# First cross-attention: query and output products between score halves, biases as bf16 rows, separate maxima per half

## The chip, the cores and the metric

The kernel runs on one core of a Trainium2 chip. The metric is the device time of one execution in microseconds (us). Engines are named as in the profile: PE is TensorE (matmul), PEld its weight loads, DVE is VectorE, ACT is ScalarE, POOL is GpSimd, SP issues the transfers.

## The reference

The program is a Perceiver-like stack of four layers, each a cross-attention, a self-attention and a feed-forward block. The change touches the first block alone, a quantised cross-attention with 16 heads of 16 channels. The 16x64 rows of x (1024) attend to all 16x128 rows of the context (2048), in one batch:

```python
q = (x @ Wq + bq).reshape(1, B * N, H, hd)
kv = (cond @ Wkv + bkv).reshape(1, -1, 2, H, hd)
q = _fq_sym(q * scale, axis=-1)       # round to 127 steps, per row and head
k = _fq_sym(k, axis=-1)
v = _fq_sym(v, axis=2)                # per channel, over all keys
attn = softmax(einsum('bhqd,bhkd->bhqk', q, k))
attn = _fq_unsigned(attn, axis=-1)    # round to 255 steps of the row's maximum
out = einsum('bhqk,bhkd->bhqd', attn, v)
return out @ Wp + bp
...
x = x + _L0_xattn_ref(_layernorm(x, axis=-1), ctx_2048, ...)
```

## The kernel before

The block `l0_xattn` fills the first 500 us of the program. Each engine runs a program of its own, in the order in which the code issues it; semaphores ("signals" in the code) order the engines against each other. Nothing is reordered by a scheduler.

**Start (to 76 us).** PE makes the values (`values`) and then the keys in 8 sets (`keys`, L1082 to L1089). Each half of a set begins with a product of a row of ones and the bias row `bk`, both fp32, that puts the bias in PSUM; two fp32 products with `wk` are added. DVE rounds the keys, POOL splits them into three bf16 parts (L1299 to L1306), PE transposes the parts, ACT copies them into `kT`. After its first work POOL has nothing to do until the first rounded set.

**Scores (76 to 486 us).** The 1024 rows are 8 tiles of 128 rows. A tile goes through 16 heads, and a head's scores are 128x2048, in one PSUM tile `s_ps` of two halves. Each engine's `tile_steps` runs a loop over i = 0 to 15; tile 0 and the last tile stand outside the hardware loop, and differ in what they leave out. In step i:

- PE: `score(t, i + 1)` makes the two halves of the next head, two 512-column products each (L1139). A half may be overwritten when DVE has taken the same half of the head before (`scores_taken`). Then `mix(t, i - 4)` multiplies the transposed weights of a head by its values, 16 small products (L1147). Behind that, in certain steps, stand products of the neighbouring tiles: `turn_out(t-1)` (i=5), `project_out(t-1)` and the transposition of the next tile's normalised rows (i=7), `queries(t+1)` (i=9), `turn_queries(t+1)` (i=13). Those with a bias begin with the fp32 product of ones and the bias row.
- DVE: `take_scores(t, i + 1)` copies each half to `ex` and takes its maximum (L1413 and L1416; each is followed by a readout of the accumulator, which is what signals `scores_taken`). The second pass starts its maximum from the first one's result `first_max`, so it waits for the first pass's own readout (`dve.wait_ge(scores_taken.sem, ...)` just ahead of it). Around the passes stand the works for other tiles: `totals` (i=1), `divide_out` (i=4), the next tile's layer norm (i=4 and 6), `add_out` (i=8), `round_queries` (i=11). Each ends with a wait for its own result, ahead of the next pass.
- POOL: `shift` makes the bias of the exponential, one operation on 128x1 (L1319); in step 5 it also makes the next tile's 1/sqrt(var).
- ACT: one exponential of 128x2048 per head (L1238), and copies: the transposed queries (`take_queries`, after heads 14 and 0), the transposed output (6), the normalised rows (8).
- SP: one transposing DMA per head moves the rounded weights (`pb`) to `pt`; `ex`, `pb` and `pt` have four slots each.

## Time and profile before

| | us |
|---|---|
| median of 3 runs | 3743.81 |
| lowest, highest | 3738.99, 3747.11 |
| the profiled execution | 3749.25 |
| its span | 3747.5 |
| the block of the change, from the profile | 0 to 500 |
| of it the eight tiles | 77.1 to 486 |

Over the whole span PE is busy 81%, DVE 61%, ACT 40%, POOL 14%. These shares average blocks with different limits, and say nothing on this one. The chain of work that ended last holds only the last 0.6 us, since it breaks at the ends of blocks. So the tiles are read from the list of groups by line, the waits, the stretches of single tiles and the order of time. All eight tiles have the same pattern. The profiled execution's time is 1.75 us longer than its span, and 5.4 us above the median of the runs. In the section with the rows, a row of a stretch gives its ends, its length, the busy time of PE, PEld, DVE, ACT and POOL with their instructions, PE's granted clock as a share of full speed, the share of the DMA engines and GB/s.

### The profile page before, as it was taken

The numbers are of one execution on the slowest core, as the hardware profiler recorded it, in microseconds if no ns is written. First come the engines' busy times: TensorE is split into PE (matmuls) and PEld (weight loads), VectorE is DVE, ScalarE is ACT, GpSimd is POOL, SyncE is SP. The second block draws the span as 40 slices with busy tenths as digits, with TensorE's granted clock in tenths as the row PEclk, the third lists the DMA queues.
The fourth block names the chain that finished last, engine by engine and source line by source line (L and its number), as shares of the span: only waits on it lengthen the run. The fifth ranks groups of instructions, "written<-read, shape, count | busy, mean of one in ns | idle before, by whom it ended". The sixth has DMA issues, their size and how long they took to land. (4 is left out here: it accounts for less than half of the span.)

```text
span 3747.5 us, 63586 instructions
## 1 busy us (share of the span) xinstructions
PE 3031.9 (81%) x23988; PEld 2108.2 (56%) x24036; DVE 2278.8 (61%) x4830; ACT 1506.0 (40%) x3074; POOL 535.2 (14%) x791
## 2 busy tenths in 40 slices
PE   7677789988776888857996868789898978787878
PEld 3333368867664556534664435355555556676767
DVE  6888844442558888865655732367777754444453
ACT  4777721111346455443442112155545532223332
POOL 3101000000002222111110022222212111111000
PEclk8766689988887776768998979899999988898787
DMA  4877740000010000010002040000000021000000
GB/s 125 164 159 164 160 135 0 0 22 0 14 56 2 2 2 2 2 69 9 6 12 69 0 135 22 3 4 3 3 6 3 3 87 51 1 0 0 1 1 12
DMA packets 316495, 141.38 MB, mean 38 GB/s; under 512 B 296221, under 2 KB 305953, under 8 KB 312613
## 3 DMA queue, kind: packets, MB, share of 16 engines
q1 hardware_dynamic: 308072, 138.45, 13.7%
q8 instruction: 126, 2.06, 0.2%
q10 hardware_dynamic: 8256, 0.52, 0.2%
q14 instruction: 41, 0.34, 0.0%
HBM read 67.65 MB, written 3.15 MB: 19 GB/s over the span
## 5 line engine op out<-in xcount | busy, mean ns | idle before, releaser
L1238 ACT ACTIVATE l0x_pb<-l0x_ex,l0x_neg_max,l0x_q_scale 128x2048 uint16<-128x2048 f32 x128 | 267.8, 2093 | 108.2 <-POOL l0x_neg_max L1319 106.5
L1139 PE MATMUL l0x_s_ps<-l0x_kT,l0x_qT 128*128 128x512 bf16 x466 | 206.5, 539 | 111.3 <-DVE l0x_ex L1416 51.8
L1413 DVE TENSOR_SCALAR_CACHE_REDUCE l0x_ex<-l0x_s_ps 128x1024 f32<-128x1024 f32 x128 | 156.4, 1222 | 46.1 <-PE l0x_s_ps L1139 35.0
L1416 DVE TENSOR_SCALAR_CACHE_REDUCE l0x_ex<-l0x_s_ps,l0x_first_max 128x1024 f32<-128x1024 f32 x128 | 164.3, 1284 | 16.7 <-DVE l0x_ex L1413 0.5
L1139 PEld LDWEIGHTS l0x_s_ps<-l0x_kT,l0x_qT 128*128 128x128 bf16 x512 | 39.2, 111 | 204.8 <-DVE l0x_ex L1416 140.5
L263 PE MATMUL l3x_bank<-l3x_w_kv_x,l3x_ctxT 128*128 128x512 f32 x256 | 120.1, 613 | 26.6 <-ACT l3x_ctx_k L762 15.8
L1147 PEld LDWEIGHTS l0x_o_ps<-l0x_v,l0x_vT 128*128 128x128 f16 x2048 | 78.6, 104 | 59.1 <-issue 41.8
L2198 PEld LDWEIGHTS l1a_bank<-l1a_u,l1a_gm 64*64 64x64 f32 x2048 | 95.5, 194 | 15.6 <-issue 14.8
L2190 PE MATMUL l1a_bank<-l1a_r,l1a_r 32*64 32x64 f32 x2048 | 75.9, 287 | 35.0 <-DVE l1a_r L2532 33.6
L263 PE MATMUL l2f_bank<-l2f_w,l2f_ln_yT 128*128 128x352 f32 x256 | 103.5, 539 | 0.0
L2198 PE MATMUL l1a_bank<-l1a_u,l1a_gm 64*64 64x8 f32 x2048 | 98.4, 235 | 4.7 <-DVE l1a_gm L2551 4.7
L2179 PE MATMUL l1a_bank<-l1a_steps,l1a_after 128*128 128x512 f32 x128 | 99.1, 866 | 0.0
L2190 PEld LDWEIGHTS l1a_bank<-l1a_r,l1a_r 32*64 32x64 f32 x2048 | 69.4, 166 | 46.6 <-DVE l1a_r L2532 37.9
L3681 PE MATMUL l3x_bank<-l3x_wproj,l3x_cat 128*128 128x256 bf16 x768 | 91.9, 278 | 4.1 <-DVE l3x_cat L3553 4.1
L679 DVE SCALAR_TENSOR_TENSOR l2f_moe_act<-l2f_bank,l2f_moe_cw,l2f_moe_sg 128x176 f32<-128x176 f32 x64 | 24.9, 400 | 114.8 <-ACT l2f_moe_sg L664 114.3
L263 PEld LDWEIGHTS l3x_bank<-l3x_w_kv_x,l3x_ctxT 128*128 128x128 f32 x256 | 46.6, 192 | 81.2 <-issue 56.7
L2191 PE MATMUL l1a_bank<-l1a_r,l1a_r 32*64 32x64 f32 x2048 | 76.6, 264 | 13.3 <-issue 13.1
L707 PE MATMUL l3x_bank<-ident,l3x_rows 128*128 128x128 f32 x448 | 64.4, 281 | 27.6 <-ACT l3x_rows L755 27.6
L3681 PEld LDWEIGHTS l3x_bank<-l3x_wproj,l3x_cat 128*128 128x128 bf16 x768 | 74.7, 100 | 20.9 <-issue 6.7
L1319 POOL TENSOR_SCALAR l0x_neg_max<-l0x_mx,l0x_q_neg 128x1 f32<-128x1 f32 x128 | 34.0, 265 | 346.6 <-DVE l0x_ex L1416 321.3
L1147 PE MATMUL l0x_o_ps<-l0x_v,l0x_vT 128*128 128x16 f16 x2048 | 75.2, 174 | 5.8 <-DMA l0x_vT<-l0x_pb 5.8
L654 PE MATMUL l2f_bank<-l2f_w,l2f_moe_actT 128*128 128x256 f32 (+1 forms) x256 | 78.6, 408 | 0.0
(747 smaller groups left out, 7838.0 us busy)
## 6 DMA issues: line engine op xcount, KB each, us to landing
l2f_wproj_raw<-in_L_xattn_wproj SPq DMA_DIRECT2D x2, 2048.0 KB, 12.3
l3a_w<-in_L_attn_W SPq DMA_DIRECT2D x4, 1024.0 KB, 11.3
l2f_w<-in_L_ffn_w SPq DMA_DIRECT2D x1, 2816.0 KB, 11.6
l0x_ex<-in_ctxT SPq DMA_DIRECT2D x8, 256.0 KB, 5.0
l0a_wq<-in_L_attn_W_Q SPq DMA_DIRECT2D x1, 2048.0 KB
l0a_wk<-in_L_attn_W_K SPq DMA_DIRECT2D x1, 2048.0 KB
l0x_vT<-l0x_pb SPq DMA_TRANSPOSE x128, 3.6
l0a_wv<-in_L_attn_W_V SPq DMA_DIRECT2D x1, 2048.0 KB, 7.8
```

The costliest lines, as they stand in the source:

```text
L263: ins = nc.tensor.matmul(out, wT(c), rhs(c), start=start and n == 0, stop=stop and n == chunks - 1)
L654: ins = nc.tensor.matmul(self.y, self.actT[0:w, e % 2, n, :], self.w_out[0:w, e, n, :], start=(e == 0 and n == 0), stop=(e == E - 1 and n ...
L1139: ins = mm(s_ps[:, j * 512:(j + 1) * 512], qT[:, h, :], kT[:, h // 2, j * 512:(j + 1) * 512], start=True, stop=True)
L1147: ins = mm(o_ps[:, h * HD:(h + 1) * HD], pt[:, h % 4, j * P:(j + 1) * P], vv[:, j, h * HD:(h + 1) * HD], start=j == 0, stop=j == KT - 1)
L1238: s.activation(pb[:, h % 4, :], ex[:, h % 4, :], ACT.Exp, scale=q_scale[:, h:h + 1], bias=nb[:, h:h + 1], accum_out=sums[:, h:h + 1]).then ...
L1413: v.tensor_scalar(ex[:, h % 4, 0:1024], s_ps[:, 0:1024], 1.0, None, ALU.mult, ALU.max, accum_out=first_max[:, h:h + 1]).then_inc(o.up(scor ...
L1416: v.tensor_scalar(ex[:, h % 4, 1024:2048], s_ps[:, 1024:2048], 1.0, first_max[:, h:h + 1], ALU.mult, ALU.max, accum_out=mx[:, h:h + 1]).th ...
L2179: ins = mm(bank[4 + j][:], after[:], flat(steps_[:, 8 * j:8 * j + 8, :]), start=False, stop=True)
L2190: mm(out, r1[0][r, 8 * half + j, tok], r1[1][r, 8 * half + j, tok], start=True, stop=False)
L2191: ins = mm(out, r2[0][r, 8 * half + j, tok], r2[1][r, 8 * half + j, tok], start=False, stop=True)
L2198: ins = mm(bank[6][r, h * HP:(h + 1) * HP], gm[r, h, :], u[r, h * HP:(h + 1) * HP], start=True, stop=True)
L3681: ins = nc.tensor.matmul(y_bank, cat[:, 8 * (n % 2) + c, :], wproj[:, 8 * n + c, i, :], start=n % 2 == 0 and c + i == 0, stop=n % 2 == 1 a ...
```

## The change

**Order.** In `score` the caller can hand in a generator that is advanced once after each half. `queries(t+1)` goes between the halves of head 8 (step i=7, before i=9 behind the mix), `project_out(t-1)` between the halves of head 10 (i=9, before i=7 behind the mix). The transposition of the next tile's rows moves from i=7 to i=3, `turn_queries` from 13 to 10. On DVE the norm moves from (4, 6) to (0, 2), `round_queries` from 11 to 8, `add_out` from 8 to 11; on ACT the norm's copy moves from 8 to 4 and the copy of the first half of the queries from 14 to 12; on POOL the norm moves from 5 to 1.

**Maxima.** The two passes write `low_max` and `high_max`, and the second doesn't wait for the first. POOL's `shift` becomes two operations on 128x1, the second waiting for the first.

**Waits.** The works between the DVE passes no longer wait for their own last result; `divide_out` waits for `totals_ready` instead.

**Biases.** The three bias vectors come as one array of 3x768 fp32 (six weight transfers in place of eight). POOL splits it at the start into three bf16 rows whose sum is the bias, in 11 operations on 3x768, and PE waits for them ahead of the first keys. Each bias product becomes one of bf16 with three rows.

```diff
+    for dst, name in ((wv, "Wv"), (bv, "bv"), (b3, "b3"), (wk, "Wk"), (wq, "Wq"), (wp, "Wp")):
...
-                mm(misc[:, 0:D], env.ones_row[:, 0:P], bq[:], start=True, stop=False)
-                project(nc, misc[:, 0:D], lambda c: norm.yT[:, c, :], lambda c: wq[:, c, :], DC, start=False).then_inc(q_ps.sem, 1)
+                mm(misc[:, 0:D], ones3[:], bq, start=True, stop=False)
+                for c in reversed(range(DC)):
+                    ins = mm(misc[:, 0:D], norm.yT[:, c, :], wq[:, c, :], start=False, stop=c == 0)
+                    if c == 0:
+                        ins.then_inc(q_ps.sem, 1)
+                    yield
...
+            pe.wait_ge(biases_set.sem, biases_set.value())
...
                     ins.then_inc(scores_ps.sem, 1)
+                    if between is not None:
+                        next(between)
...
+                    between = queries(t + 1) if more and i == 7 else project_out(t - 1) if before and i == 9 else None
...
+            for n in range(3):
+                src = b_sum if n else b3
+                pool.sem_inc(first.up(), 1)
+                g.tensor_copy(b_part[:], src[:]).then_inc(first.up(), 1)
+                pool.wait_ge(first.sem, first.at())
+                if n < 2:
+                    g.tensor_tensor(b_sum[:], src[:], b_part[:], ALU.subtract).then_inc(first.up(), 1)
+                    pool.wait_ge(first.sem, first.at())
+                pool.sem_inc(first.up(), 1)
+                g.tensor_scalar(b_part[:], b_part[:], env.ident[0:3, n:n + 1], 0.0, ALU.mult, ALU.add).then_inc(first.up(), 1)
...
-                g.tensor_scalar(nb[:, h:h + 1], mx[:, h:h + 1], q_neg[:, h:h + 1], LN255, ALU.mult, ALU.add).then_inc(o.up(shifted), 1)
+                g.tensor_scalar(mx[:, h:h + 1], low_max[:, h:h + 1], high_max[:, h:h + 1], q_neg[:, h:h + 1], ALU.max, ALU.mult).then_inc(o.up(), 1)
+                pool.wait_ge(o.sem, o.at())
+                pool.sem_inc(o.up(), 1)
+                g.tensor_scalar(nb[:, h:h + 1], mx[:, h:h + 1], 1.0, LN255, ALU.mult, ALU.add).then_inc(o.up(shifted), 1)
...
-                dve.wait_ge(scores_taken.sem, scores_taken.value(t, 2 * h + 1))
-                v.tensor_scalar(ex[:, h % 4, 1024:2048], s_ps[:, 1024:2048], 1.0, first_max[:, h:h + 1], ALU.mult, ALU.max, accum_out=mx[:, h:h + 1]).then_inc(o.up(scores_taken), 1)
+                v.tensor_scalar(ex[:, h % 4, 1024:2048], s_ps[:, 1024:2048], 1.0, None, ALU.mult, ALU.max, accum_out=high_max[:, h:h + 1]).then_inc(o.up(scores_taken), 1)
...
-                o.eng.wait_ge(tile_done.sem, o.at(tile_done))
```

How PE's order moves is read from three places in the looped tile. First, PE before, in steps 7 to 9: the score products of head 8 are the first row, L1158 and the L263 behind it are `project_out`, L241 the transposition of the normalised rows, L1102 and its L263 `queries`.

```order
L1139 MATMUL l0x_s_ps<-l0x_kT,l0x_qT 128x512 x2
L1147 MATMUL l0x_o_ps<-l0x_v,l0x_vT 128x16 x16
L1158 MATMUL l0x_t_ps<-l0x_bp,ones_row 128x256
L263 MATMUL l0x_t_ps<-l0x_wp,l0x_oT 128x256 x2
L239 REGISTER_ALU
L241 MATMUL l0x_misc<-ident,l0x_ln_y 128x128 x2
L1135 REGISTER_ALU
L1139 MATMUL l0x_s_ps<-l0x_kT,l0x_qT 128x512 x2
```

Everything of the neighbouring tiles stands in a row behind the mix, ahead of the first half of head 9. PE after, in step 7 (L1105 and L1107 are `queries`, L1146 the score products, L1156 the mix):

```order
L1146 MATMUL l0x_s_ps<-l0x_kT,l0x_qT 128x512 x2
L1105 MATMUL l0x_misc<-l0x_b_rows,l0x_ones3 128x256
L1107 MATMUL l0x_misc<-l0x_wq,l0x_ln_yT 128x256
L1142 REGISTER_ALU
L1146 MATMUL l0x_s_ps<-l0x_kT,l0x_qT 128x512 x2
L1107 MATMUL l0x_misc<-l0x_wq,l0x_ln_yT 128x256
L1156 MATMUL l0x_o_ps<-l0x_v,l0x_vT 128x16 x16
```

The bias and one product stand behind the first half, the other product behind the second. `project_out` has the same form in step 9. DVE before, the two passes of a head with what each waits for:

```order
L1413 TENSOR_SCALAR l0x_ex,l0x_first_max<-l0x_s_ps 128x1024 [waits l0x_scores_ps]
L1414 REGISTER_ALU
L1416 TENSOR_SCALAR l0x_ex,l0x_mx<-l0x_s_ps,l0x_first_max 128x1024 [waits l0x_scores_taken,l0x_scores_ps]
L1427 TENSOR_TENSOR l0x_o_rows<-l0x_o_ps,l0x_total 128x256 [waits l0x_mixed]
L1409 REGISTER_ALU [waits l0x_o_ready]
```

And DVE after, at the same place:

```order
L1443 TENSOR_SCALAR l0x_ex,l0x_low_max<-l0x_s_ps 128x1024 [waits l0x_scores_ps]
L1444 REGISTER_ALU
L1445 TENSOR_SCALAR l0x_ex,l0x_high_max<-l0x_s_ps 128x1024 [waits l0x_scores_ps]
L1456 TENSOR_TENSOR l0x_o_rows<-l0x_o_ps,l0x_total 128x256 [waits l0x_totals_ready,l0x_mixed]
L1439 REGISTER_ALU
```

The wait for `scores_taken`, a result of DVE itself, is gone from the second pass, and the wait for `o_ready` from behind the division.

## Rows read from the trace of the kernel before

**Rows 1.** Stretches: tile 0, first and sixth of the looped tiles, last tile.

```profile
77.10:124.70 47.60, 32.79 (x253) 12.79 (x256) 42.08 (x74) 35.10 (x34) 5.18 (x19) 0.72 0.83 162
124.70:178.30 53.60, 38.50 (x339) 19.12 (x344) 43.47 (x77) 37.94 (x42) 5.17 (x19) 0.69 0.73 155
...
387.90:442.00 54.10, 41.55 (x339) 19.67 (x344) 43.47 (x77) 38.24 (x42) 5.17 (x19) 0.63 0.68 155
442.00:486.00 44.00, 31.11 (x354) 15.33 (x356) 40.55 (x68) 36.11 (x38) 4.01 (x15) 0.81 0.92 184
```

**Rows 2.** Order of time, DVE in tile 2: start us, duration, what, [idle before].

```profile
186.75 1.22 DVE L1413 TENSOR_SCALAR_CACHE_REDUCE l0x_ex<-l0x_s_ps 128x1024 f32<-128x1024 f32 x1
187.90 0.08 DVE L1413 DVE_READ_ACCUMULATOR l0x_ex<-l0x_s_ps 128x1 f32 x1
188.11 1.28 DVE L1416 TENSOR_SCALAR_CACHE_REDUCE l0x_ex<-l0x_s_ps,l0x_first_max 128x1024 f32<-128x1024 f32 x1
...
189.32 1.22 DVE L1413 TENSOR_SCALAR_CACHE_REDUCE l0x_ex<-l0x_s_ps 128x1024 f32<-128x1024 f32 x1
...
192.53 1.23 DVE L1413 TENSOR_SCALAR_CACHE_REDUCE l0x_ex<-l0x_s_ps 128x1024 f32<-128x1024 f32 x1 [0.23 <-DVE l0x_o_rows L1427]
```

**Rows 3.** Waits of the six looped tiles: total us, times, longest us.

```profile
DVE l0x_ex L1413 <- PE l0x_s_ps L1139: 23.1, 19, 2.5
...
PE l0x_s_ps L1139 <- ACT l0x_qT L1210: 13.2, 6, 2.4
```

**Rows 4.** Order of time, PE's score products beside rows 2.

```profile
186.89 1.03 PE L1139 MATMUL l0x_s_ps<-l0x_kT,l0x_qT 128*128 128x512 bf16 x2 [0.39 <-DVE l0x_ex L1416]
...
188.19 1.01 PE L1139 MATMUL l0x_s_ps<-l0x_kT,l0x_qT 128*128 128x512 bf16 x2
```

**Rows 5.** Order of time, PE and DVE at the end of tile 2.

```profile
225.00 1.53 PE L1139 MATMUL l0x_s_ps<-l0x_kT,l0x_qT 128*128 128x512 bf16 x3
...
226.10 1.23 DVE L1413 TENSOR_SCALAR_CACHE_REDUCE l0x_ex<-l0x_s_ps 128x1024 f32<-128x1024 f32 x1 [0.70 <-PE l0x_s_ps L1139]
...
230.32 1.22 DVE L1413 TENSOR_SCALAR_CACHE_REDUCE l0x_ex<-l0x_s_ps 128x1024 f32<-128x1024 f32 x1 [1.56 <-PE l0x_s_ps L1139]
```

**Rows 6.** Order of time, the query products in tile 2, lower clock.

```profile
208.82 1.13 PE L1102 MATMUL l0x_misc<-l0x_bq,ones_row 1*128 1x256 f32 x2
...
209.88 2.08 PE L263 MATMUL l0x_misc<-l0x_wq,l0x_ln_yT 128*128 128x256 f32 x4
...
211.74 1.91 PE L1139 MATMUL l0x_s_ps<-l0x_kT,l0x_qT 128*128 128x512 bf16 x4
...
212.84 1.22 DVE L1413 TENSOR_SCALAR_CACHE_REDUCE l0x_ex<-l0x_s_ps 128x1024 f32<-128x1024 f32 x1 [2.44 <-PE l0x_s_ps L1139]
```

**Rows 7.** Order of time, the query products in tile 0, upper clock.

```profile
105.65 1.13 PE L263 MATMUL l0x_misc<-l0x_wq,l0x_ln_yT 128*128 128x256 f32 x4
```

**Rows 8.** POOL's operation on 128x1, from the page.

```profile
L1319 POOL TENSOR_SCALAR l0x_neg_max<-l0x_mx,l0x_q_neg 128x1 f32<-128x1 f32 x128 | 34.0, 265 | 346.6 <-DVE l0x_ex L1416 321.3
```

**Rows 9.** POOL's groups by line and shape: busy us, mean ns, idle before.

```profile
L3589 POOL TENSOR_TENSOR l3x_wproj<-l2f_wproj_raw,l3x_wproj 128x1024 bf16<-128x1024 f32 x8 | 17.0, 2122 | 0.6
L1301 POOL TENSOR_TENSOR l0x_k_rest<-l0x_k_num,l0x_k_parts 128x512 f32<-128x512 f32 x8 | 9.2, 1154 | 0.6
...
L3587 POOL CAST l3x_wproj<-l2f_wproj_raw 128x1024 bf16<-128x1024 f32 x8 | 8.3, 1042 | 0.5
...
L1304 POOL CAST l0x_k_parts<-l0x_k_rest 128x512 bf16<-128x512 f32 x8 | 4.9, 610 | 1.3 <-POOLq L1303 1.3
```

**Rows 10.** Order of time, POOL in the start.

```profile
9.99 0.56 POOL L232 TENSOR_TENSOR l0x_ln_rstd<-l0x_ln_ve,neg_half 128x1 f32<-128x1 f32 x1
```

**Rows 11.** Order of time, the first keys.

```profile
26.55 0.69 PE L1087 MATMUL l0x_s_ps<-l0x_bk,ones_row 1*128 1x256 f32 x2
...
30.03 0.69 DVE L1355 TENSOR_REDUCE l0x_k_row<-l0x_s_ps 128x32 f32<-128x512 f32 x1 [1.58 <-PE l0x_s_ps L263]
```

**Rows 12.** A small operation of DVE among the keys: min/median/max ns.

```profile
L1357 DVE TENSOR_SCALAR l0x_k_row<-l0x_k_row x8: 180/239/1105, 30.8 to 64.9; 128x32 f32<-128x32 f32 x8
```

**Rows 13.** The first score pass by line: min/median/max ns.

```profile
L1413 DVE TENSOR_SCALAR_CACHE_REDUCE l0x_ex<-l0x_s_ps x128: 1218/1224/1226, 77.1 to 483.3; 128x1024 f32<-128x1024 f32 x128
```

More of the change, by code:

```diff
@@ L1086, in keys @@
                     out, first = k_bank[n % 2][:, b * D:(b + 1) * D], n * CH + b * SC
-                    mm(out, env.ones_row[:, 0:P], bk[:], start=True, stop=False)
+                    mm(out, ones3[:], bk, start=True, stop=False)
                     ins = project(nc, out, lambda c: ctxT[:, c, first:first + SC], lambda c: wk[:, c, :], DC, start=False)
@@ L1118, in _ @@
                 if n == 2:
-                    queries(0)
+                    whole(queries(0))
                 if n >= 2:
@@ L1127, in _, with score @@
             pe.wait_ge(qT_taken.sem, qT_taken.value(0))
-            def score(t, h, first=False):
+            def score(t, h, first=False, between=None):
                 if not first and h % 8 == 0:
@@ L1157, in project_out @@
                 pe.wait_ge(oT_taken.sem, oT_taken.value(t))
-                mm(out_bank[:, D:2 * D], env.ones_row[:, 0:P], bp[:], start=True, stop=False)
-                project(nc, out_bank[:, D:2 * D], lambda c: oT[:, c, :], lambda c: wp[:, c, :], DC, start=False).then_inc(y_ps.sem, 1)
+                mm(out_bank[:, D:2 * D], ones3[:], bp, start=True, stop=False)
+                for c in reversed(range(DC)):
+                    ins = mm(out_bank[:, D:2 * D], oT[:, c, :], wp[:, c, :], start=False, stop=c == 0)
+                    if c == 0:
+                        ins.then_inc(y_ps.sem, 1)
+                    yield
             def tile_steps(t, before, more):
                 for i in range(H):
+                    between = queries(t + 1) if more and i == 7 else project_out(t - 1) if before and i == 9 else None
                     if i + 1 < H:
-                        score(t, i + 1)
+                        score(t, i + 1, between=between)
                     elif more:
@@ L1172, in tile_steps @@
                         mix(t - 1, H + i - 4, before)
+                    if more and i == 3:
+                        pe.wait_ge(qT_taken.sem, qT_taken.value(t))
+                        whole(norm.tensor(pe, t + 1, misc))
                     if before and i == 5:
                         turn_out(t - 1)
-                    if before and i == 7:
-                        project_out(t - 1)
-                    if more and i == 7:
-                        whole(norm.tensor(pe, t + 1, misc))
-                    if more and i == 9:
-                        queries(t + 1)
-                    if more and i == 13:
+                    if more and i == 10:
                         turn_queries(t + 1)
@@ L1193, in _ @@
             turn_out(last)
-            project_out(last)
+            whole(project_out(last))
         @block.scalar
@@ L1256, in tile_steps @@
                         take_queries(o, 1)
-                    if before and i == 6:
-                        take_out(o, t - 1)
-                    if more and i == 8:
+                    if more and i == 4:
                         o.t = t + 1
@@ L1262, in tile_steps @@
                         o.t = t
-                    if more and i == 14:
+                    if before and i == 6:
+                        take_out(o, t - 1)
+                    if more and i == 12:
                         act.wait_ge(qT_ps.sem, qT_ps.value(t + 1))
```

51 lines of the change are left out of this document (30 added, 21 removed).

## The prediction

> **What bounds the kernel now.** I read the stretches first, one per tile. Tile 0 takes 47.6 us, the six looped tiles 317.3 us together (124.7 to 442.0), which is 52.9 us each, and the last 44.0 us [rows 1]. In a looped tile DVE is busy 43.5 us and no other engine more. The reader is to see two things in that row: DVE is the fullest engine, and 9.4 us of the tile are not DVE work.
>
> The order of time of DVE shows a plain head, one with nothing else in it [rows 2]: the first pass starts at 186.75 and the next head's first pass at 189.32, so 2.57 us per head. The first pass starts its readout 1.15 us after its own start (187.90), which ends at 187.98; the second pass starts only at 188.11, 1.36 us after the first. From there to the next first pass are 1.21 us: nothing stands between those two, and that pass starts together with the readout. Sixteen plain heads are 41.1 us. So 11.8 us of a looped tile are insertions of DVE and waits.
>
> DVE's insertions: of the 43.5 us busy, 16 heads of 2.44 us (1.23 from 186.75 to 187.98, and 1.21) are 39.0, which leaves 4.5 us, and after each of five insertions DVE idles 0.23 us until its own result has come back (192.53) [rows 2]. The list of waits shows the rest: the first pass waits 23.1 us in six tiles for a score product, 3.9 us a tile, and PE in turn waits 13.2 us for ACT's copy of the queries, 2.2 a tile [rows 3].
>
> **The change part by part.** All of it is summed against the profiled execution, 3749.25 us.
>
> *The two passes.* Without the wait the second pass can start as the first one's readout does, 1.15 us after the first, as the first pass does behind the second. Its duration of 1.28 us becomes the first one's 1.22, since it takes the same form; so its readout comes at 1.15 in place of 1.21. DVE alone then needs 2.30 us for a head, 0.27 less. What is late next is PE. I work out its loop at the lower of its clock's two levels, 1.2 GHz. A second-half product starts at 186.89, 0.06 us after the readout that frees its half; the mix follows, and the next first-half product starts at 188.19, 1.30 us later [rows 4]. A product started at 225.00 lets the pass start at 226.10, 1.10 us later [rows 5]. Around the loop: first pass to its successor 1.15, that one's readout and release 1.15 + 0.08 + 0.06, product to product 1.30, product to pass 1.10: 4.84 us for two heads, 2.42 us for one. At the upper level, 2.4 GHz, the products take half, and DVE's 2.30 stands. The granted clock was 0.69 in the first looped tile and 0.63 in the sixth [rows 1], so about a third of the time at the upper level: 2.38 us per head. It hides nothing else; PE's slack is gone at the lower clock, and each product inserted on PE there is paid in full.
>
> *The waits behind the insertions.* Five per looped tile by 0.23 us is 1.15 us less. With the gaps inside the insertions (their operations still wait for each other) DVE's own additions become about 4.7 us a tile: 4.5 busy, 1.0 of gaps that stay, less 0.8 by which neighbours overlap their ends, 0.07 us each.
>
> *The queries.* Before: bias 1.13 us and products 2.08 us by their records, at the lower clock, and the first pass behind them is 2.44 us late. By starts (208.82 for the bias, 211.74 for the next score product) they hold PE 2.9 us [rows 6]. After: the bias is one bf16 pass of 256 columns, which I price at half a score product (four end 1.91 us after the first one's start [rows 6], some 0.43 each), 0.2 us; the products stay at four passes, 1.7. Between the halves they delay the second-half product by 0.75 us (3.20 in place of 2.45 after the head's start), and the second product and the mix delay the next first half; together I get 1.6 us late at the lower clock. At the upper clock the four product passes end 1.13 us after the first one's start [rows 7], two of them about 0.5: that between halves fits in the 1.15 us of a pass, so nothing is late.
>
> *The output product* has the same size, and now stands in the step where DVE runs `round_queries` (2.0 us) between two passes. PE has then 2 us of slack: nothing is late in the looped tiles. In the last tile nothing covers it, and it costs like the queries, up to 1.6 us. `add_out`, one step later, doesn't wait.
>
> *The smaller PE insertions.* `turn_queries` makes the pass 0.70 us late now [rows 5]; behind it `add_out` stands on DVE, 0.4 us, so 0.4 remains at the lower clock. `turn_out` has lost the layer norm that covered it: 0.5. The transposition in step 3 lies beside `divide_out`: 0.05. Upper clock: nothing. So the waits for PE come to 2.5 us a tile at the lower clock and 0 at the upper, 1.7 for a third at the upper.
>
> *The copy of the queries* at head 12 in place of 14 comes two heads before it is needed. The pass that was 1.56 us late [rows 5] is on time. What else waits on ACT: a head takes ACT 2.1 us, and the tile's 38.3 us busy [rows 1] fit in 44. Nothing is late on SP, whose transfers are moved past by none of the edits.
>
> *POOL's second operation* costs 0.27 us by its like [rows 8] and a wait of 0.1 to 0.3, once per head, in the chain DVE, POOL, ACT, transfer, mix. That chain has four slots. I take it at nothing for the tiles: the cover is the three heads, 7 us, between the exponential and the pass that needs its slot. At the very end it shows once, 0.4 us, against 0.9 us that the bf16 bias saves in the last output product.
>
> A looped tile after: 16 x 2.38 + 4.7 + 1.7 = 44.5 us in place of 52.9. Six save 50.4. Tile 0: 16 x 2.38 is 38.1, and 0.8 + 0.2 for the norm, 1.1 queries, 1.8 rounding, 0.5 turning: 42.5 in place of 47.6, 5.1 saved. The last: 38.1 + 0.5 + 0.5 + 1.1: 40.2, 3.8 saved. Tail 0.5.
>
> *The start.* POOL's 11 operations have no row at 3x768. The nearest are casts (0.61 at 512 columns, 1.04 at 1024) and two-input operations (1.15 and 2.12) [rows 9]; midway, 0.83 and 1.64. Four copies, four two-input and three scaled ones of either price are 12.4 to 14.8 us, with ten gaps 13.2 to 15.6. At the 512 prices all would be 9.4, at 2.12 for each 23.3. POOL is free at 10.6 [rows 10], so the biases are ready at 24 to 26.3, and the keys start at 26.55 [rows 11]: just in time. Then two short biases bring the first rounding, for which DVE waited at 30.03, 0.6 us forward. I take 0.6 gained; the ends are 0.6 gained and 7.5 lost (34.0 less 26.5). Two fewer transfers I take at nothing.
>
> Sum: 50.4 + 5.1 + 3.8 + 0.5 + 0.6 = 60.4 us, so 3688.9 against the profiled execution. That one is 5.4 us above the median of the runs, so against the median: 3743.8 - 60.4 = **3683.4 us**, a saving of 1.6%.
>
> **The rivals.** *Upper clock.* Denser products keep PE at the upper level: a looped tile is 16 x 2.30 + 4.7 = 41.5 us, 11.4 less, in all about 80: 3664. For it: plain heads come closer together. Against it: the fp32 bias passes go, and the granted clock was 0.63 to 0.72 in tiles with more of them [rows 1]. The Trainium skill, "TensorE: Matmul & The Clock Gate", section "What's actually happening", says that the clock is low by default and that activity lifts it; by that rule this rival is possible, and its opposite too.
>
> *Lower clock throughout.* 16 x 2.42 + 4.7 + 2.5 = 45.9: 42 + 4 + 3 + 1 = 50 saved, 3694.
>
> *The head's time stays at 2.57*, because the product of the second half, not the readout, sets the second pass: at 186.89 + 1.10 = 187.99 it was ready for the pass of 188.11, only 0.12 us before [rows 2, 4]. Then 128 x 0.19 = 24 us of the gain are missing: 3707.
>
> *The biases are late* by up to 7.5 us in place of 0.6 gained: 3691.
>
> *Slower.* POOL now works twice per head beside the passes. If a pass waited while POOL holds something that both need, each of the two operations would add 0.27: 128 x 0.54 = 69 us, 3752. It decides from 0.47 us per head (60.4 / 128). For it: among the keys a small DVE operation takes 180 to 1105 ns [rows 12], the long ones beside POOL's two-input work. Against it: all 128 first passes lie within 1218 and 1226 ns [rows 13], though POOL's operation falls into each. The Trainium skill, "SBUF — State Buffer", section "Who interferes with whom", names this lock between the two engines, but excepts the form of operation that also writes an accumulator; by that rule, which agrees with the 8 ns spread, the passes are safe and only small operations are not.
>
> **How the numbers follow.** Forecast with the mixed clock 0.55; upper clock 0.14; lower throughout 0.12; head's time stays 0.10; biases late 0.05; slower 0.04. A measurement of this kernel can tell about 0.2%, 7.5 us. All but the last are faster: 0.95; within 0.2% 0.01; slower 0.04. The forecast's own spread is some 10 us, a third of the clock's share either way and the unknown gaps; the range of 3664 to 3708 takes in all cases but the slower one, its ends being the upper clock and the unchanged head.
>
> **What would show it.** In the changed profile: plain heads 2.30 to 2.42 us apart, the second pass 1.15 us behind the first and 1.22 long; no wait of PE for ACT's copy at the tile's end; DVE's wait for the score products near 1.7 us a tile, most of it at the head with the queries; looped tiles of 42 to 46 us; POOL's last bias operation done before 26.5. It is wrong if the second pass is still 1.3 us behind, if the tile is above 47, or if time appears outside the first 500 us, where nothing is touched.

## The result, and the profile after

The changed kernel takes 3694.07 us (median of 4 runs, 3688.57 to 3697.23) against 3742.96 for the kernel before on the same chip: a ratio of 0.9867, 95% interval 0.9854 to 0.9880, 48.9 us saved. The profiled execution took 3693.92 us with a span of 3692.1; between the two profiled executions the span fell by 55.4 us. That is 6.5 us more than the medians say, since the profiled execution of the kernel before was 6.3 us above its median and that of the changed kernel 0.2 below. The forecast was 60.4 saved and 3683.4 us. The time lies in the range and on the right side, but two of the prediction's steps failed in opposite directions, as the experiments show.

The first group is from the page of the kernel after: the span, and the granted clock in 40 slices (tenths of full speed).

```profile
span 3692.1 us, 63817 instructions
...
PEclk8899799988977777679998798899999988898787
```

Each slice is 92 us, so the first attention is the first four to five. Next its stretches, one per tile: tile 0, the first, third and sixth of the looped tiles, the last one (busy us and instructions of PE, PEld, DVE, ACT and POOL, then granted clock, DMA share, GB/s). They answer to [rows 1].

```profile
74.90:115.80 40.90, 30.58 (x255) 11.80 (x253) 39.88 (x74) 32.06 (x32) 9.19 (x32) 0.79 0.93 160
115.80:159.10 43.30, 31.16 (x343) 14.37 (x344) 40.64 (x79) 38.89 (x42) 10.71 (x38) 0.90 1.15 187
200.60:241.60 41.00, 30.25 (x342) 15.29 (x342) 40.57 (x78) 37.59 (x42) 9.94 (x35) 0.92 1.10 205
...
323.60:364.60 41.00, 30.34 (x342) 15.29 (x342) 40.57 (x78) 37.60 (x42) 9.94 (x35) 0.92 1.11 208
364.60:405.50 40.90, 30.57 (x325) 13.20 (x325) 38.41 (x70) 37.66 (x39) 9.21 (x33) 0.83 1.13 196
```

From the third on a looped tile takes 41.0 us, the first two 43.3 and 41.5; before all six took 52 to 54. DVE is busy for 40.57 of the 41.0, so it now has hardly a gap. The granted clock is 0.92 (0.90 and 0.86 in the first two) where it was 0.63 to 0.70, and PE's records add up to 30 us where they were 37 to 42. The eight tiles together take 330.6 us in place of 408.9.

DVE's order of time in the third looped tile answers to [rows 2]: start, duration, what.

```profile
227.57 1.22 DVE L1443 TENSOR_SCALAR_CACHE_REDUCE l0x_ex<-l0x_s_ps 128x1024 f32<-128x1024 f32 x1
228.72 0.08 DVE L1443 DVE_READ_ACCUMULATOR l0x_ex<-l0x_s_ps 128x1 f32 x1
228.72 1.22 DVE L1445 TENSOR_SCALAR_CACHE_REDUCE l0x_ex<-l0x_s_ps 128x1024 f32<-128x1024 f32 x1
229.86 0.08 DVE L1445 DVE_READ_ACCUMULATOR l0x_ex<-l0x_s_ps 128x1 f32 x1
229.86 1.22 DVE L1443 TENSOR_SCALAR_CACHE_REDUCE l0x_ex<-l0x_s_ps 128x1024 f32<-128x1024 f32 x1
```

The second pass starts with the first one's readout, 1.15 us behind it, and takes 1.22; the next head follows after 1.14: 2.29 us for a head. All waits of DVE in the six looped tiles (total us, times, longest) answer to [rows 3]:

```profile
DVE l0x_ex L1443 <- PE l0x_s_ps L1146: 2.7, 3, 2.0
DVE l0x_ln_mv L209 <- DVEq L208: 0.9, 6, 0.2
```

The 23.1 us of waits for a score product are 2.7, the waits behind the insertions are gone, and no wait of PE for ScalarE's copy of the queries is left in this stretch. The longest wait, 2.0 us at the end of the first looped tile, has another cause: PE there waits 2.1 us for a transposed head, and the score product stands behind that in its order:

```profile
157.64 0.59 PE L1156 MATMUL l0x_o_ps<-l0x_v,l0x_vT 128*128 128x16 f16 x16 [2.13 <-DMA l0x_vT<-l0x_pb]
...
159.14 1.23 DVE L1443 TENSOR_SCALAR_CACHE_REDUCE l0x_ex<-l0x_s_ps 128x1024 f32<-128x1024 f32 x1 [2.00 <-PE l0x_s_ps L1146]
```

**Where the 55.4 us are.** Block by block, from PE's first instruction to its last: this attention fell from 487.7 to 411.5 us (76.2 saved), the Mamba block l1a from 486.9 to 482.6; but the last layer's cross-attention l3x rose from 650.1 to 668.3 and its attention l3a from 347.2 to 352.6, where no line was changed. All other blocks are within 1 us. So some 24 us are given back between 2336 and 3368 us. Each block's time comes from one trace, and the same code differs a little from trace to trace: the eight tiles of the kernel before took 408.9 us in one and 405.7 in another (the run with 209 idle instructions below), those of the changed kernel 330.5 to 332.4 in six.

In l3x the same instructions run in the same order on every engine. The two traces stay within 0.4 us of each other until the end of the first turn of DVE's loop. DVE there, kernel after:

```profile
2466.13 1.22 DVE L959 TENSOR_REDUCE l3x_self_sum<-l3x_e 128x16 f32<-128x1024 f32 x1 [3.18 <-ACT l3x_e L939]
2468.34 0.25 DVE L961 RECIPROCAL l3x_self_inv<-l3x_self_sum 128x16 f32<-128x16 f32 x1 [1.00 <-DVE l3x_self_sum L959]
```

And the kernel before, at the same place:

```profile
2544.47 1.22 DVE L958 TENSOR_REDUCE l3x_self_sum<-l3x_e 128x16 f32<-128x1024 f32 x1 [2.38 <-ACT l3x_e L938]
2545.73 0.25 DVE L960 RECIPROCAL l3x_self_inv<-l3x_self_sum 128x16 f32<-128x16 f32 x1
```

The view names ScalarE as what ended the idle time, but ScalarE's exponential came no later. What stands between, and is not counted as busy, is the branch that closes DVE's loop. The trace's own records of it say: the branch ends, and the next instruction of DVE starts 0.24 to 0.26 us later before, 2.75 to 2.97 us later after, six times in l3x, and once in l3a (0.24 and 2.90). The reciprocal, ready as before, comes 1.00 us late once more (1.00 to 1.23 in the six turns). The transfers of the queues that bring instructions, in the stretch 2463.2 to 2468.4 of the kernel after:

```profile
DMA packets 2, 0.02 MB, mean 3 GB/s; under 512 B 0, under 2 KB 0, under 8 KB 0
...
q14 instruction: 2, 0.02, 1.1%
```

The same stretch of the kernel before (2542.3 to 2546) has no packet at all. Over the whole of l3x this queue moved 6 packets before and 35 after. In each of the six turns of the loop it moved 5, the first some 1 us behind the branch. I read this as DVE fetching code at each turn. In the compiled programs that of DVE is 47 instructions shorter after the change (2720 in place of 2767: the second pass's wait is gone 48 times, once for each head in the three copies of the tile's code, and the new order adds one), so every loop behind the first attention lies elsewhere. The experiments begin with this.

### The profile page after: what moved, and what is told of

Same layout as the page of the kernel before. It is cut to its first block and busy times, and to the rows that moved or that the text cites. A ratio compares the mean times of both kernels' runs of the same rounds, so it can differ in the third digit from the quotient of the medians.

```text
span 3692.1 us, 63817 instructions
## 1 busy us (share of the span) xinstructions
PE 2963.2 (80%) x24004; PEld 2073.1 (56%) x24004; DVE 2257.9 (61%) x4830; ACT 1502.9 (41%) x3074; POOL 585.9 (16%) x931
## 5 line engine op out<-in xcount | busy, mean ns | idle before, releaser
L1247 ACT ACTIVATE l0x_pb<-l0x_ex,l0x_neg_max,l0x_q_scale 128x2048 uint16<-128x2048 f32 x128 | 267.2, 2088 | 35.1 <-POOL l0x_neg_max L1350 23.5
L1146 PE MATMUL l0x_s_ps<-l0x_kT,l0x_qT 128*128 128x512 bf16 x512 | 178.3, 440 | 76.5 <-DVE l0x_ex L1445 41.1
L1443 DVE TENSOR_SCALAR_CACHE_REDUCE l0x_ex<-l0x_s_ps 128x1024 f32<-128x1024 f32 x128 | 156.2, 1220 | 14.3 <-PE l0x_s_ps L1146 13.3
L1445 DVE TENSOR_SCALAR_CACHE_REDUCE l0x_ex<-l0x_s_ps 128x1024 f32<-128x1024 f32 x128 | 156.1, 1220 | 0.0
L264 PE MATMUL l3x_bank<-l3x_w_kv_x,l3x_ctxT 128*128 128x512 f32 x256 | 127.4, 644 | 24.7 <-ACT l3x_ctx_k L763 14.4
L1146 PEld LDWEIGHTS l0x_s_ps<-l0x_kT,l0x_qT 128*128 128x128 bf16 x512 | 33.4, 101 | 155.8 <-DVE l0x_ex L1445 105.8
L1156 PEld LDWEIGHTS l0x_o_ps<-l0x_v,l0x_vT 128*128 128x128 f16 x2048 | 71.2, 99 | 60.6 <-DMA l0x_vT<-l0x_pb 31.6
L2217 PE MATMUL l1a_bank<-l1a_r,l1a_r 32*64 32x64 f32 x2048 | 71.0, 279 | 39.8 <-DVE l1a_r L2559 35.6
L2206 PE MATMUL l1a_bank<-l1a_steps,l1a_after 128*128 128x512 f32 x128 | 89.9, 792 | 0.0
L1156 PE MATMUL l0x_o_ps<-l0x_v,l0x_vT 128*128 128x16 f16 x2048 | 72.3, 171 | 19.3 <-DMA l0x_vT<-l0x_pb 19.3
L1347 POOL TENSOR_SCALAR l0x_mx<-l0x_low_max,l0x_high_max,l0x_q_neg 128x1 f32<-128x1 f32 x128 | 47.5, 371 | 215.0 <-DVE l0x_ex L1445 198.9
L708 PEld LDWEIGHTS l3x_bank<-ident,l3x_rows 128*128 128x128 f32 x448 | 49.8, 142 | 55.3 <-ACT l3x_rows L756 50.0
```

The lines of the kernel that those rows point to most:

```text
L264: ins = nc.tensor.matmul(out, wT(c), rhs(c), start=start and n == 0, stop=stop and n == chunks - 1)
L708: ins = self.L.nc.tensor.transpose(self.banks[u][:, h * P:(h + 1) * P], self.rows[:, 4 * u + h, :], self.L.env.ident[:])
L1146: ins = mm(s_ps[:, j * 512:(j + 1) * 512], qT[:, h, :], kT[:, h // 2, j * 512:(j + 1) * 512], start=True, stop=True)
L1156: ins = mm(o_ps[:, h * HD:(h + 1) * HD], pt[:, h % 4, j * P:(j + 1) * P], vv[:, j, h * HD:(h + 1) * HD], start=j == 0, stop=j == KT - 1)
L1247: s.activation(pb[:, h % 4, :], ex[:, h % 4, :], ACT.Exp, scale=q_scale[:, h:h + 1], bias=nb[:, h:h + 1], accum_out=sums[:, h:h + 1]).then ...
L1443: v.tensor_scalar(ex[:, h % 4, 0:1024], s_ps[:, 0:1024], 1.0, None, ALU.mult, ALU.max, accum_out=low_max[:, h:h + 1]).then_inc(o.up(scores ...
```

## Experiments

### The give-back: where DVE's code lies

Six runs move DVE's program and nothing else. The filler is a semaphore increment that nobody waits for, ahead of the first wait of DVE's program, where DVE idles until 8.9 us:

```diff
+            filler = L.sem("filler")
+            for _ in range(47):
+                dve.sem_inc(filler, 1)
             dve.wait_ge(env.own.sem, env.own.value())
             first = Order(dve, L.sem("dve_first_order"))
```

**47 instructions in the changed kernel**

> The changed kernel with 47 one-word semaphore increments put at the head of VectorE's program, where VectorE waits for its first input anyway; every later instruction of VectorE then stands as far from the program's start as in the kernel before, and nothing else differs. Theory (place of the code): in the changed kernel VectorE needs 2.75 to 2.97 us behind each of the six loop branches of l3x and one of l3a, where the kernel before needed 0.24, because its program is 47 instructions shorter; so these gaps return to 0.24, l3x falls from 668 to 650 us, l3a from 352.6 to 347, and the whole from 3694 to about 3670. Rival (clock): the blocks start some 79 us earlier, so their work falls otherwise on the moments at which TensorE's clock is granted; then a delay of nothing changes nothing: l3x stays near 668, the whole at 3694, the gaps at 2.8.

Measured: 3669.48 us (5 runs, 3666.61 to 3674.63), ratio to before 0.9799 (0.9785 to 0.9813). The gaps behind the branches are 0.24, l3x took 649.7 us and l3a 347.3. The queue and the wait in l3x:

```profile
DVE l3x_self_sum L959 <- ACT l3x_e L939: 18.7, 8, 2.4
...
q14 instruction: 6, 0.05, 0.0%
```

Adding 47 instructions that do nothing made the kernel 24.6 us faster. l3x started at 2337.5 us here and at 2335.7 in the changed kernel, so the moment is not the cause. The run with 32 instructions below says it more sharply: its l3x starts at 2335.8 us, within 0.1 us of the changed kernel's, and takes 650.1 us in place of 668.3.

**209 instructions in the kernel before**

The same lines with 209 in place of 47, in the kernel before.

> The kernel before with 209 such increments at the head of VectorE's program, so that each later instruction stands 209 behind its old place, which is 256 less 47: by the Trainium skill, Advanced Engine Details and Errata, ISA Cache, an engine holds two lines of 256 instructions, and modulo 256 the code then lies as in the changed kernel. Theory (place of the code, in steps of 256): the seven gaps go from 0.24 to about 2.8 us, l3x from 650 to 668, l3a from 347 to 352, in all +24 us and up to 8 us more in the first block, where the increments take longer than VectorE's wait. Rival one (clock only): l3x stays at 650. Rival two (place, but not in steps of 256): gaps of some loops change, of others than these.

Measured: 3776.02 us (ratio 1.0083, 1.0067 to 1.0098), 30.2 more. The gaps in l3x are 2.81, in l3a 2.71; l3x took 668.3 us, l3a 349.1. The first block took 6.2 us more (493.9): the increments put the first score pass 9.4 us later, and the tiles took 3 us less in this trace. The waits and the queue in l3x:

```profile
DVE l3x_self_sum L958 <- ACT l3x_e L938: 20.4, 7, 3.3
...
DVE l3x_self_inv L960 <- issue: 6.6, 6, 1.3
...
DVE l3x_self_sum L958 <- issue: 3.4, 1, 3.4
...
q14 instruction: 35, 0.29, 0.1%
```

The loss of l3x is produced in the kernel before too, without any part of the change. A clock that only looks at the moment is out: l3x starts at 2421 here, 7 us from where it took 650.

**16 and 32 instructions in the changed kernel**

> The changed kernel with 16 increments at the head of VectorE's program. By the Trainium skill, Advanced Engine Details and Errata, ISA Cache, two lines of 256 instructions are held: a loop is then slow only where it touches three lines. The loop of l3x is 271 instructions long, which puts the slow positions of its start into a stretch of 15; in the changed kernel and in the run with the passes alone it started one instruction apart, both slow. Theory (three lines touched): 16 instructions on it is past this stretch, and l3x is fast, with gaps of 0.24 and 650 us. Rival (something wider, such as a line fetched ahead that pushes out the loop's first): still slow, 2.8 us and 668. The loop of l3a (312 long) is slow by the rule in a stretch of 57 and may be either.

> The same with 32 increments. Theory (three lines touched): l3x fast, 650. Rival (a wider stretch): slow or fast, which tells where between 16 and 47 it ends. Whole 3670 or 3694 by which of the two it is.

Measured: 3673.25 and 3670.13 us, one run each. With 16, l3x is fast (gaps 0.24, 650.0 us) and l3a still has its gap (3.05), though its block shows nothing of it (346.9 us). With 32 both are fast (0.24; 650.1 and 347.1). The rule under test, that of the first expectation above, was that code is held in lines of 256 instructions, two at a time, and that a loop is slow where it touches three. A loop that is moved on then turns fast when its start reaches the next line, so two such edges lie a multiple of 256 apart. It would explain each loop by itself, but not both: in the compiled program their starts are 372 instructions apart, the one passes its edge between 0 and 16, the other between 16 and 32, so the edges are 373 to 403 apart, and no multiple of 256 lies in that. One of 128 does, 384.

**128 and 59 instructions in the changed kernel**

> The changed kernel with 128 increments at the head of VectorE's program. What the runs with 0, 16, 32 and 47 showed: the loop of l3x slow at 0 and fast from 16 on, that of l3a slow at 0 and 16 and fast from 32 on, though the two starts are 372 instructions apart. No step of 256 fits both edges, one of 128 does (three lines of 128 held, a loop slow where it touches four): the packets of the instruction queue are 8.2 KB each. Theory (step of 128): everything lies as in the changed kernel, l3x and l3a are slow again, gaps of 2.8, l3x 668, l3a 352 and the whole near 3698, a few us more for the increments. Rival (step of 256, as the Trainium skill's section ISA Cache has it): l3x is fast, 650, and the whole 3672 to 3680.

> The same with 59 increments, 12 more than the run with 47. Theory (step of 128): a loop of 275 instructions, that of l3f, which was fast in all runs so far, now touches four lines: its one branch, 0.26 to 0.29 us so far, takes 2.6 to 3.0, while l3x and l3a stay fast (0.24, 650 and 347). Rival (any other rule): l3f stays at 0.26 to 0.29. Whole 3670 to 3675 either way.

Measured with 128: 3703.96 us (one run), gaps 2.82 and 2.80, l3x 668.3, l3a 349.1, and 10.6 us more in the first block. Its queue in l3x:

```profile
q14 instruction: 35, 0.29, 0.1%
```

So a step of 256 alone is out, and one of 128 fits: the packets of this queue are 8192 bytes, and the compiled program of 2720 instructions is 174,080 bytes, 64 for each, so one packet holds 128. It isn't shown that the pattern repeats every 128: between 59 and 256 only 128 was run, and a single wide slow stretch would give the same rows. The Trainium skill, "Advanced Engine Details and Errata", section "ISA Cache", has the right kind of rule, two cache lines of 256 instructions; the step that these runs show is finer. With 59: 3672.53 us (one run), l3x and l3a fast as expected, but l3f's branch took 0.28, not 2.6 to 3.0. That forecast failed: what decides a slow loop is not fully told by "four lines of 128".

All runs together, by how far DVE's code lies behind its place in the changed kernel (gap: us from the branch's end to the next instruction, mean):

```
shift  kernel                          gap l3x  l3x us  gap l3a  l3a us
  -1   before, separate maxima alone    2.79    667.6    2.71    350.4
   0   changed                          2.86    668.3    2.90    352.6
   0   changed, fp32 bias rows          2.79    668.4    2.72    352.6
  16   changed + 16                     0.24    650.0    3.05    346.9
  32   changed + 32                     0.24    650.1    0.24    347.1
  47   changed + 47                     0.24    649.7    0.24    347.3
  47   before                           0.24    650.1    0.24    347.2
  48   changed, joined maximum          0.24    650.0    0.24    348.0
  48   before, order alone              0.24    650.1    0.24    347.1
  59   changed + 59                     0.24    649.9    0.23    347.1
 128   changed + 128                    2.82    668.3    2.80    349.1
 256   before + 209                     2.81    668.3    2.71    349.1
```

The last two experiments below, with shift 0, took 668.6 and 668.8 us in l3x.

How 2.6 us become 3 per turn: DVE would have waited 2.38 us for ScalarE at this place anyway, so of the 2.5 added only 0.8 show (3.18), and 1.0 at the reciprocal. That is 1.8 in this turn and 11.8 in all six, and PE's idle time in l3x rose by as much, from 80.6 to 92.1 us. PE's records add up to 576.2 us in place of 569.5: 6.7 us more, at the lower level of the clock for 64 us of the block in place of 50. Line, form, busy us and mean ns of the kernel after:

```profile
L264 PE MATMUL l3x_bank<-l3x_w_kv_x,l3x_ctxT 128*128 128x512 f32 x256 | 127.4, 644 | 24.7 <-ACT l3x_ctx_k L763 14.4 <-ACT l3x_ctx_q L763 10.3
```

And of the changed kernel with 47 instructions, the same work:

```profile
L264 PE MATMUL l3x_bank<-l3x_w_kv_x,l3x_ctxT 128*128 128x512 f32 x256 | 120.1, 612 | 27.6 <-ACT l3x_ctx_k L763 15.8 <-ACT l3x_ctx_q L763 11.8
```

The 11.5 idle and the 6.7 busy are the 18.2 us. That the late turns are what lowered the clock is not shown by itself; it went down in the slow runs (0.95) and in none of the fast ones (0.96).

### The gain: which part of the change brings what

**The separate maxima alone, in the kernel before**

```diff
-                dve.wait_ge(scores_taken.sem, scores_taken.value(t, 2 * h + 1))
-                v.tensor_scalar(ex[...], s_ps[:, 1024:2048], 1.0, first_max[:, h:h + 1], ALU.mult, ALU.max, accum_out=mx[:, h:h + 1])
+                v.tensor_scalar(ex[...], s_ps[:, 1024:2048], 1.0, None, ALU.mult, ALU.max, accum_out=high_max[:, h:h + 1])
...
-                g.tensor_scalar(nb[...], mx[...], q_neg[...], LN255, ALU.mult, ALU.add).then_inc(o.up(shifted), 1)
+                g.tensor_scalar(mx[...], first_max[...], high_max[...], q_neg[...], ALU.max, ALU.mult).then_inc(o.up(), 1)
+                g.tensor_scalar(nb[...], mx[...], 1.0, LN255, ALU.mult, ALU.add).then_inc(o.up(shifted), 1)
```

> The kernel before with only the separate maxima: the second pass takes no operand of the first and waits for nothing of VectorE, GpSimd does two operations per head; order and fp32 bias rows as before. Theory (head): VectorE's plain head falls from 2.57 to 2.42 at the lower clock and 2.30 at the upper; with the clock unchanged near 0.71 l0x falls by 16 x 8 x 0.15 to 0.27, 19 to 34 us, from 488 to 454 to 469. Rival (the closer passes raise TensorE's clock by themselves): the granted clock of l0x is above 0.8 and l0x is 435 or less. VectorE's program is 48 instructions shorter, so by the theory on the place of the code l3x is at 668 here too, with no other change near it: the whole then gains only 0 to 15 us.

Measured: 3745.36 us, ratio 1.0007 (0.9996 to 1.0019): nothing. Block by block it is not nothing: this attention fell by 28.4 us to 459.3 (clock 0.76 in place of 0.71, from PE's first instruction in the block to its last, as below), and l3x rose to 667.6 and l3a to 350.4. Plain heads are 2.29 us at the upper clock and 2.36 at the lower. Whoever had timed this edit alone would have dropped more than a third of the gain.

**The joined maximum again, in the changed kernel**

The reverse of the diff above.

> The changed kernel with the joined maximum again: the second pass takes the first one's maximum and waits for it, GpSimd does one operation per head; order and bf16 bias rows stay changed. Theory (the order and the biases raise the clock, the passes shorten the head): plain heads 2.50 to 2.57 us, clock of l0x still above 0.8, l0x 411 plus 128 x 0.21 to 0.28, 438 to 447. Rival (only close passes keep TensorE at the upper clock): the clock falls to 0.75 or less and l0x is 455 or more. VectorE's program has one instruction more than before, so l3x is at 650 by the theory on the place of the code.

Measured: 3696.4 us, ratio 0.9872 (0.9857 to 0.9887), as good as the changed kernel. This attention took 442.0 us (clock 0.78; plain heads 2.56 at either clock), 30.5 more than there, and l3x 650.0. The trace also holds 6 us of luck: the untouched block l1x took 150.1 us in it and 156 to 157 in all others, with shorter records of PE. The clock fell between what the two theories said: neither part alone lifts it to 0.87.

**The bias rows in fp32, in the changed kernel**

```diff
-        bq, bk, bp = (b_rows[:, n * D:(n + 1) * D] for n in range(3))
+        bq, bk, bp = (b3[0:1, n * D:(n + 1) * D] for n in range(3))
...
-                mm(misc[:, 0:D], ones3[:], bq, start=True, stop=False)
+                mm(misc[:, 0:D], env.ones_row[:, 0:P], bq, start=True, stop=False)
```

> The changed kernel with the bias rows in fp32 again (taken from the first of the three loaded rows, one product of one row each); GpSimd's eleven operations at the start fall away; maxima and order stay changed. Theory (the biases are a small term): two bias products per tile cost 0.3 to 0.8 us more each and lie beside a pass or round_queries for the most part, the keys at the start some 1 to 2 us; the clock of l0x stays at 0.83 or more and l0x at 413 to 420 us, the whole within 0.2% of the changed kernel. Rival (the short biases are what lifts the clock): 0.78 or less and l0x 430 or more. VectorE's program is as long as in the changed kernel, so l3x is at 668.

Measured: 3696.26 us, ratio 0.9870 (0.9853 to 0.9886); 416.3 us in this block (clock 0.88). The first pass starts at 77.2 in place of 74.9, and the head behind the queries takes 2.59 in place of 2.29, seven times: 2.3 and 2.1 of the 4.8 us. The biases are a small term here and don't carry the clock.

**The order alone, in the kernel before**

The joined maximum and the fp32 rows, all else as changed.

> The kernel before with the changed order alone: query and output products between the halves, the moved steps, the waits behind the insertions gone; joined maximum, one operation of GpSimd per head, fp32 bias rows. Theory (order and passes add up, biases small): l0x 442 to 450, near the 442 of the run with order and biases, clock 0.75 to 0.78, plain heads 2.57; the whole near 3700. Rival (the biases carry a part of the 46 us that order and biases brought together): l0x 455 or more. VectorE's program has one instruction more than before: l3x at 650, branch gaps of 0.24.

Measured: 3708.96 us, ratio 0.9907 (0.9891 to 0.9924). This block 452.6 us (clock 0.77), 35.1 less than before, between the two expectations; l3x 650.1. Against the run with the joined maximum the bf16 biases are worth 10.6 us, more than the 4.8 in the changed kernel. This order includes the waits behind the insertions, which no run takes by themselves. The four combinations of maxima with order and biases in this block are 487.7 (before), 459.3 (maxima), 442.0 (order and biases) and 411.5 (all): 28.4 and 45.7 by themselves, 76.2 together, so they add up but for 2 us.

**The turning and the copy of the queries at their old steps**

```diff
-                    if more and i == 10:
+                    if more and i == 13:
                         turn_queries(t + 1)
...
-                    if more and i == 12:
+                    if more and i == 14:
                         act.wait_ge(qT_ps.sem, qT_ps.value(t + 1))
                         take_queries(o, 0)
```

> The changed kernel with the turning of the queries and ScalarE's copy of them back at their old steps, 13 and 14 in place of 10 and 12. Theory (the copy is worth what the last head waited): ScalarE gets to the copy behind its exponential of head 14, so the first product of the next tile waits for it as in the kernel before: the last head of a tile takes 3.7 to 4.3 us in place of 2.29, seven times 1.4 to 2.0, and l0x goes from 411.5 to 421 to 426, with a little more where the wait lowers the clock. Rival (with the shorter head and the high clock the copy has slack anyway): l0x 411 to 414. VectorE's program is as long as in the changed kernel, l3x stays at 668: whole 3704 to 3710, or 3694.

Measured: 3714.24 us, ratio 0.9914 (0.9898 to 0.9931); this block 431.6, 20.1 more, beyond the 10 to 15 expected; l3x 668.6. The end of the second looped tile:

```profile
206.34 1.19 ACT L1219 ACTIVATE l0x_qT<-l0x_misc 64x512 bf16<-64x512 bf16 x2
...
207.66 1.88 PE L1146 MATMUL l0x_s_ps<-l0x_kT,l0x_qT 128*128 128x512 bf16 x4 [3.36 <-ACT l0x_qT L1219]
208.72 1.23 DVE L1443 TENSOR_SCALAR_CACHE_REDUCE l0x_ex<-l0x_s_ps 128x1024 f32<-128x1024 f32 x1 [3.18 <-PE l0x_s_ps L1146]
```

The last head takes 5.56 us in place of 2.29, seven times 3.3. ScalarE is further behind when the copy comes (its exponential starts 1.0 us behind the end of the second pass, before the change 0.5), and the heads are shorter, so the same misplaced step costs more than the 1.56 it cost before [rows 5]. This move is the largest piece of the reordering that was taken back by itself.

**The products of queries and output in a row behind the mix**

```diff
-                        score(t, i + 1, between=between)
+                        score(t, i + 1)
...
+                    if between is not None:
+                        whole(between)
```

> The changed kernel with the bias and both products of the queries, and those of the output, in a row behind the mix of steps 7 and 9, as before the change, the step numbers and all else as changed. Theory (between the halves they are hidden at the upper clock, in a row they delay the next first half by what exceeds TensorE's slack): queries 0.28 + 1.13 us at the upper clock against some 0.5 of slack, 0.9 us late in seven tiles, the output product hidden by round_queries: l0x 411.5 plus 6, 417 to 420. Rival one (TensorE has slack enough at the upper clock): 411 to 413. Rival two (the longer wait lowers the clock, and that costs more than the products): 425 or more and the clock of l0x 0.82 or less. l3x stays at 668.

Measured: 3693.29 us, ratio 0.9856 (0.9839 to 0.9873), against 3694.07 for the changed kernel: no difference that can be told. In the block it is 4.6 us (416.1), with the clock at 0.87. The late pass behind the queries, in the third looped tile of this run:

```profile
225.44 1.22 DVE L1445 TENSOR_SCALAR_CACHE_REDUCE l0x_ex<-l0x_s_ps 128x1024 f32<-128x1024 f32 x1 [0.50 <-PE l0x_s_ps L1146]
```

That head takes 2.87 us in place of 2.29 in five of the six looped tiles, and 3.25 in the other: the move on which the diff spends most lines is worth some 4 us of the block, at most.

## Why the prediction was right, and where it was not

- **The two passes: right.** 1.15 behind, 1.22 long, 2.30 forecast and 2.29 measured at the upper clock. At the lower one I had PE late by a loop of 2.42 over two heads. Where plain heads follow each other at this level, the first five of tile 0 with the maxima alone, they take 2.43, 2.36, 2.36, 2.45 and 2.45, mean 2.41; one by itself takes 2.36, since it waits only for its own release and product (1.29 and 1.07). That the second-half product holds the head at 2.57 was refuted.
- **The share of the clock: the step that failed in the block.** I took the upper clock for a third of the time, by [rows 1]. A granted clock of 0.92 in the looped tiles is the upper level for five sixths of it. By my own working a tile is then 16 x 2.30 + 4.7 = 41.5; it is 41.0. So the rival "upper clock" happened, with a saving of 76.2 us against its 80, and I had given it 0.14. The error was to take the clock as given while removing the waits on which it hung: over the block, maxima alone gave 0.76, order alone 0.77, all together 0.87. Why just the sum of them lifts it so far is seen, not explained.
- **The insertions: right.** 41.0 less 16 x 2.29 is 4.4 us a tile (4.7 forecast) with all five trailing waits gone; what the waits are worth alone was not measured.
- **Queries and output product: right in kind.** At the upper clock nothing is late, as the fp32 and the in-a-row runs show by what comes back (0.3 and 0.6 us a tile).
- **The copy of the queries: the right step, sized too small.** 1.56 us was what it cost at the old pace; at the new one it is 3.3 a tile, 20 us in all.
- **GpSimd's second operation: right.** It takes 0.19 us and the first 0.37; no pass waits for it, and the passes kept their 1.22, so the lock of the slower rival did not show.
- **The tail: wrong.** I had it 0.5 us shorter. From the end of the last tile's stretch, 405.5, to the end of the block at 422.1 are 16.6 us, before 12.3 (486.0 to 498.3). The last division starts 9.2 us behind ScalarE's last exponential, before 4.6: it waits for transposed heads. The transfers that transpose them (min, median, max ns), kernel after:

```profile
L1068 SPq DMA_TRANSPOSE l0x_vT<-l0x_pb x128: 1702/2382/3622, 80.5 to 412.8; - x128
```

  Before, the median was 1623 ns. In the last tile each starts 0.1 us behind the end of the one before it, where there were 0.1 to 1.8 us between them, mostly 0.9. I had written that nothing is late on SP, and that the chain of four slots costs the tiles nothing; the 2.0 us at the end of the first looped tile are its cost there. Tiles 78.3 and start 2.2 saved, 4.3 lost here: 76.2.
- **The start: right on the critical point.** The biases were ready at 24.7 us, in the window of 24 to 26.3, the first keys at 26.2. It gained 2.2 us, not 0.6, since each of the eight sets has two shorter biases; the fp32 run gives 2.3. (The 9.4 us that I gave for all operations at the 512-column prices should have been 8.9 to 10.5; nothing rests on it.)
- **What the prediction named as a sign of being wrong: time outside the first 500 us.** It came: 18.2 and 5.4 us, by the place of DVE's code. None of my rivals had it, since I costed only instructions that run, and not where those that don't change come to lie. Two more of its signs were off, both by the clock: looped tiles of 41.0 us in place of 42 to 46, and 0.45 us a tile of DVE's waits for the score products in place of 1.7. Between the two traces the sum is 76 less 24, and 4 more for l1a, whose time moved between 482.6 and 487.3 through all these runs with its clock (0.70 to 0.74), less 1.5 in the rest.

So the forecast of 60.4 came within 5 us of the 55.4 between the traces through two misses of 16 and 24 us of opposite sign, which is luck; against the medians it is 11 us off, 6.5 of them because the trace of the kernel before was slower than its median. The version that these runs point to is the changed kernel with DVE's code moved: with 47 instructions that do nothing it takes 3669.48 us, 2.0% less than before and 24.6 us less than the changed kernel.

## What to carry to other kernels

Where a gain in one part comes out smaller than its own stretch of the trace shows, compare the untouched blocks one by one; if an engine resumes late behind a loop's branch, shift its program by a few dozen idle instructions before blaming the change. Price a misplaced step at the new pace, not at the old one, since the engines behind the shortened one can be further behind. And when the waits of TensorE are what is taken away, work the sum at both clocks and do not average them by the share of the kernel before.

## What the hardware showed that I had not expected

- A loop's branch on VectorE is followed by a gap of 0.24 us or of 2.7 to 3.05, by where the loop of 271 or 312 instructions lies in the program; both were slow again when moved by 128 and by 256 instructions, and each slow turn of l3x goes with 5 packets of 8192 bytes on the instruction queue. A loop of 275 instructions that should have been caught at one place was not; this is open.
- l3a paid for its one slow branch 5.4 us in the changed kernel, 3.3 with the maxima alone, 1.9 with 128 and with 209 instructions, and once nothing (346.9 us with a gap of 3.05). What decides that was not looked into.
- The separate maxima, which take 48 waits out of VectorE's program, were worth 28.4 us in their block and the code moved so that 20.7 were lost 2000 us later.
- The transposing transfers took 2382 ns (median) in place of 1623 in tiles of 41.0 us in place of 52 to 54. They are the next limit that the trace shows: in a looped tile SP's queue is busy with them for 35.5 to 36.0 of the 41.0 us, in the first one for 41.0 of 43.3, and there and at the very end PE waits for them. Whether shorter ones would shorten the block was not tried.
